# An adaLN block with windowed attention and routed experts: first tiles normalised on VectorE, products of zeros moved and widened in the first block, first steps of GpSimd and TensorE written out

## What is computed

```python
mod = (silu(c) @ wmod).reshape(4, 6, 1, 128)        # sa, ca, ga, sb, cb, gb
ga = (2 * (ga >= 0) - 1) * maximum(abs(ga), 0.25)   # gb likewise
h = layernorm(x) * (1 + ca) + sa
q, k, v = h @ Wq.T, h @ Wk.T, h @ Wv.T              # 16 heads, 4 KV heads, D = 64
scores = 30 * tanh((q @ k / 8) / 30)                # key j for query i: i - 128 < j <= i
x = x + ga * (softmax(scores) @ v @ Wo.T)
h = layernorm(x) * (1 + cb) + sb
x = x + gb * moe(h)                                 # top 1 of 8 experts, relu, 512 wide
```

## Time and profile before

| | us |
|---|---|
| median of 3 executions | 450.78 (450.40 to 451.82) |
| the profiled execution | 450.22 |
| its span, first to last instruction | 448.5 |
| TensorE busy | 422.5 (94% of the span) |
| VectorE busy | 293.8 (66%) |
| ScalarE busy | 300.1 (67%) |
| GpSimd busy | 310.1 (69%) |

### The profile page before, as it was taken

The page is one execution under the profiler, slowest core; times in us unless marked ns, Lnnn a source line. Parts: engine busy times, 40 slices in busy tenths (PEclk is TensorE's granted clock), DMA queues, the critical chain, the costliest instruction groups (busy, mean ns, idle before and its releaser), DMA issues. The chain is left out here.

```text
span 448.5 us, 14988 instructions
## 1 busy us (share of the span) xinstructions
PE 422.5 (94%) x5628; PEld 294.5 (66%) x5628; DVE 293.8 (66%) x878; ACT 300.1 (67%) x537; POOL 310.1 (69%) x495
## 2 busy tenths in 40 slices
PE   8899999999999999999999999999998856999991
PEld 4656767666767676676767675767655543799991
DVE  6475576766686868486767675775768662476751
ACT  5978586868786868777777777785856431555540
POOL 4546475868787878687878777786777884066663
PEclk9999999999999999999999999999999977899997
DMA  7663602101010210121212200202021033993110
GB/s 245 223 228 100 203 21 71 34 19 53 23 56 19 62 59 23 38 61 38 60 39 67 68 31 20 79 20 80 26 84 42 10 101 105 330 362 109 35 43 28
DMA packets 33023, 37.15 MB, mean 83 GB/s; under 512 B 3650, under 2 KB 29255, under 8 KB 32952
## 3 DMA queue, kind: packets, MB, share of 16 engines
q1 hardware_dynamic: 29448, 27.43, 20.2%
q0 software_dynamic: 3072, 8.37, 5.1%
q10 hardware_dynamic: 432, 0.40, 0.3%
HBM read 15.69 MB, written 16.91 MB: 73 GB/s over the span
## 5 line engine op out<-in xcount | busy, mean ns | idle before, releaser
L1071 DVE COPY_PREDICATED own<-before,turns 128x1024 f32<-128x1024 uint32 x56 | 68.8, 1229 | 42.6 <-PE turns L455 42.4
L1552 POOL TENSOR_TENSOR OL<-O,OH 128x512 fp32r<-128x512 f32 x64 | 81.8, 1284 | 17.5 <-ACT OH L826 17.3
L813 ACT ACTIVATE PR<-own 128x1024 f32<-128x1024 f32 x64 | 65.4, 1022 | 17.4 <-DVE own L1071 17.4
L1543 POOL TENSOR_SCALAR_AFFINE_SELECT PM<-PR 128x1024 f32<-128x1024 f32 x64 | 70.3, 1098 | 7.1 <-ACT PR L819 7.1
L819 ACT ACTIVATE PR<-PR 128x1024 f32<-128x1024 f32 x64 | 67.2, 1050 | 0.1
L451 PE MATMUL own<-Q,K 64*32 64x128 f32 (+3 forms) x896 | 58.7, 441 | 1.9 <-issue 1.4
L455 PE MATMUL turns<-Q,K 64*32 64x128 f32 (+3 forms) x896 | 57.4, 429 | 0.0
L1104 DVE TENSOR_TENSOR O<-turns,R 128x512 f32<-128x512 f32 x64 | 42.9, 682 | 16.2 <-PE turns L494 16.1
L1588 POOL DMA_INDIRECT sorted_rows<-PAY,slot_i x32 | 34.6, 1082 | 13.0 <-issue 12.4
L455 PEld LDWEIGHTS turns<-Q,K 64*32 64x32 f32 x896 | 36.6, 107 | 9.5
L799 ACT ACTIVATE Q<-turns 128x512 f32<-128x512 f32 x64 | 38.3, 600 | 5.5 <-PE turns L377 4.1
(11 more groups left out here) (201 smaller groups left out, 1041.3 us busy)
## 6 DMA issues: line engine op xcount, KB each, us to landing
sorted_rows<-empty_row SPq DMA_DIRECT2D x8, 776.0 KB, 6.5
VM<-V SPq DMA_DIRECT2D x56, 64.0 KB, 2.1
out_dram<-PAY SPq DMA_DIRECT2D x32, 64.0 KB, 1.8
w_stage<-w_dram SPq DMA_DIRECT2D x8, 256.0 KB
PR<-sorted_rows SPq DMA_DIRECT2D x2, 776.0 KB, 9.2
x_sb<-sorted_rows SPq DMA_DIRECT2D x2, 776.0 KB, 10.2
x_sb<-x_dram SPq DMA_DIRECT2D x3, 512.0 KB, 5.9
O<-w_dram SPq DMA_DIRECT2D x4, 256.0 KB, 8.5
```

Source lines behind the costliest of these rows:

```text
L813: act.activation(pr, own[:, :, :].rearrange("p a n -> p (a n)"), ACT.Tanh, scale=SCORE_SCALE).then_inc(tanhed, 1)
L1071: dve.copy_predicated(own[:, :, :].rearrange("p a (r n) -> p (a r) n", n=P), before[:, :].bitcast(U32).unsqueeze(1).to_broadcast([P, 2 * R ...
L1543: pool.affine_select(out=PM[:, u % P_RING, :].rearrange("p (r n) -> p r n", n=P), in_=PR[:, u % P_RING, :].rearrange("p (r n) -> p r n", n ...
L1552: pool.tensor_tensor(OL[:, t % 2, :, half], O[:, t % 2, :, half], OH[:, t % 2, :, half].bitcast(F32), ALU.subtract).then_inc(ol_done, 1)
```

## The change

Loads and splits: the second pair of tiles has a load of its own, ahead of the second half of the query weights; the value weights come after these. The output weights' high parts are made on VectorE (`split_both`) instead of ScalarE. First tiles: `normalise_first` on VectorE replaces `normalise1` for tiles 0 and 1, and GpSimd leaves out two of four steps for block 0. V of block 0 is copied by VectorE (`keep_v_first`), ahead of `prepare_mod`. `high_x(0)` comes ahead of the split of the first query weights. TensorE: zeros of 256 columns ahead of `turn_x(0)`, 384 instead of 128 columns ahead of `project_k(0)`, `project_q(0, 2)` ahead of `project_v(0)`. The first pass of TensorE's loop is written out, with `attend(0)` ahead of `turn_x(3)` and `score(1, 1)`, where the loop had it behind both. GpSimd's first steps are written out, with `mask(0, 0)` ahead of `rstd1_of(3)` and of `differ(1)`, and `mask(0, 1)` ahead of the last two `rstd1_of`. The measures of tiles 10 and 11 move ahead of VectorE's loop.

```diff
...
-            (WkH[:, :], WkL[:, :], stage_k), (WqH[:, :QH], WqL[:, :QH], stage_q[:, :QH]), (WvH[:, :], WvL[:, :], stage_v),
-            (WqH[:, QH:], WqL[:, QH:], stage_q[:, QH:]),
+            (WkH[:, :], WkL[:, :], stage_k), (WqH[:, :QH], WqL[:, :QH], stage_q[:, :QH]), (WqH[:, QH:], WqL[:, QH:], stage_q[:, QH:]),
+            (WvH[:, :], WvL[:, :], stage_v),
...
             sp.dma_start(stage_q[:, :QH], wq[:, :QH]).then_inc(wq0_in, 16)
+            sp.dma_start(x_sb[:, 2:4, :], x_v[0][:, 2:4, :]).then_inc(x_second, 16)
+            sp.dma_start(stage_q[:, QH:], wq[:, QH:]).then_inc(wq1_in, 16)
             sp.dma_start(stage_v, wv).then_inc(wv_in, 16)
-            sp.dma_start(stage_q[:, QH:], wq[:, QH:]).then_inc(wq1_in, 16)
-            sp.dma_start(x_sb[:, 2:BATCH_TILES, :], x_v[0][:, 2:BATCH_TILES, :]).then_inc(x_in[0], 16)
+            sp.dma_start(x_sb[:, 4:BATCH_TILES, :], x_v[0][:, 4:BATCH_TILES, :]).then_inc(x_in[0], 16)
...
+            run_idle(1, 2)
             pe.wait_ge(consts, CONSTS)
             turn_x(0)
...
-            run_idle(1, 1)
+            run_idle(1, 3)
             project_k(0)
             project_q(0, 1)
             project_q(0, 0)
+            project_q(0, 2)
             project_v(0)
-            project_q(0, 2)
             turn_x(1)
...
             score(1, 0)
+            project_v(1)
+            project_q(1, 3)
+            sums(0)
+            attend(0)
+            turn_x(3)
+            score(1, 1)
+            project_q(2, 1)
+            score(2, 0)
+            project_k(2)
+            sums(1)
+            project_q(2, 0)
+            score(2, 1)
+            attend(1)
+            project_q(2, 2)
+            score(3, 0)
-            for e in range(-10, TILES - 14, 2):
+            for e in range(-8, TILES - 14, 2):
...
             split_high(SPLIT_K)
-            normalise1(0)
-            normalise1(1)
+            high_x(0)
             split_high(SPLIT_Q0)
-            high_x(0)
-            split_high(SPLIT_V)
             act.wait_ge(rows_done, 1)
             act.activation(mod3_flat, bank["rows",][0:BATCHES, 0:3 * P], ACT.Copy).then_inc(mod_kept, 1)
             split_high(SPLIT_Q1)
+            split_high(SPLIT_V)
             keep_k(0)
...
             normalise1(3)
-            keep_v(0)
             high_x(1)
...
             normalise1(6)
-            split_high(SPLIT_O1)
-            split_high(SPLIT_O0)
+            normalise1(7)
             keep_v(1)
             weigh(1, 0)
-            normalise1(7)
             keep_q(1, 3)
...
+            def normalise_first(t):
+                dve.wait_ge(rstd1_done, 1)
+                dve.tensor_scalar(XN[:, t * P:(t + 1) * P], x_sb[:, t, :], mv1[:, t, 0:1], rstd1[:, t:t + 1],
+                                  ALU.subtract, ALU.mult).then_inc(normed1, 1)
+
+            def keep_v_first():
+                dve.wait_ge(v_projected, 1)
+                dve.tensor_copy(V[:, 0:2, :], bank["v", 0].rearrange("p (t n) -> p t n", t=2)).then_inc(v_kept, 1)
+
+            def split_both(i):
+                dve.wait_ge(split_in[i], 16)
+                dve.tensor_copy(split[i][0], split[i][2]).then_inc(weights_h, 1)
+                split_low(i)
...
             split_low(SPLIT_K)
+            normalise_first(0)
+            normalise_first(1)
             keep_columns()
             keep_gate()
-            split_low(SPLIT_Q0)
             full_x(0)
             low_x(0)
+            split_low(SPLIT_Q0)
             measure1(2)
             measure1(3)
             gather1(2)
             gather1(3)
+            split_low(SPLIT_Q1)
             split_low(SPLIT_V)
-            split_low(SPLIT_Q1)
             measure1(4)
...
             gather1(5)
+            keep_v_first()
             prepare_mod()
             full_x(1)
             low_x(1)
+            split_both(SPLIT_O1)
+            split_both(SPLIT_O0)
             measure1(6)
...
+            measure1(10)
+            measure1(11)
+            gather1(10)
+            gather1(11)
...
-                if e == 6:
-                    split_low(SPLIT_O1)
-                    split_low(SPLIT_O0)
...
-                pool.tensor_scalar(minus1[:, s], mv1[:, s, 0], -1.0, None, ALU.mult).then_inc(minus1_done, 1)
+                if k:
+                    pool.tensor_scalar(minus1[:, s], mv1[:, s, 0], -1.0, None, ALU.mult).then_inc(minus1_done, 1)
                 pool.wait_ge(var1_done, k + 1)
                 pool.tensor_tensor(rstd1[:, s], var1[:, s], neg_half[:, :], ALU.pow).then_inc(rstd1_done, 1)
+                if k == 0:
+                    return
...
-            for e in range(-12, TILES - 4, 2):
+            rstd1_of(0)
+            rstd1_of(1)
+            rstd1_of(2)
+            mask(0, 0)
+            rstd1_of(3)
+            differ(1)
+            mask(0, 1)
+            rstd1_of(4)
+            rstd1_of(5)
+            for e in range(0, TILES - 4, 2):
```

More of the change, by code:

```diff
@@ L189, in build @@
         turns = pb("turns", [P, 6, 512])
-        x_first = sem("x_first")
+        x_first, x_second = sems("x_first", "x_second")
         x_in = [sem(f"x_in{b}") for b in range(BATCHES)]
@@ L202, in build @@
         final_out = [sem(f"final_out{n}") for n in range(3)]
-        consts, banks_cleared, c_exped, c_steps, silu_done, columns_done, rows_done, mod_kept, sa_kept, ca_kept = sems(
-            "consts", "banks_cleared", "c_exped", "c_steps", "silu_done", "columns_done", "rows_done", "mod_kept", "sa_kept", "ca_kept")
+        consts, banks_cleared, c_steps, silu_done, columns_done, rows_done, mod_kept, sa_kept, ca_kept = sems(
+            "consts", "banks_cleared", "c_steps", "silu_done", "columns_done", "rows_done", "mod_kept", "sa_kept", "ca_kept")
         cb_kept, gate_parts, gates_kept, weights_h, weights_l = sems(
@@ L240, in build @@
         split = (
-            (WkH[:, :], WkL[:, :], stage_k), (WqH[:, :QH], WqL[:, :QH], stage_q[:, :QH]), (WvH[:, :], WvL[:, :], stage_v),
-            (WqH[:, QH:], WqL[:, QH:], stage_q[:, QH:]),
+            (WkH[:, :], WkL[:, :], stage_k), (WqH[:, :QH], WqL[:, :QH], stage_q[:, :QH]), (WqH[:, QH:], WqL[:, QH:], stage_q[:, QH:]),
+            (WvH[:, :], WvL[:, :], stage_v),
             (WoH[:, REP:, :], WoL[:, REP:, :], stage_o[:, REP:, :]), (WoH[:, :REP, :], WoL[:, :REP, :], stage_o[:, :REP, :]))
-        SPLIT_K, SPLIT_Q0, SPLIT_V, SPLIT_Q1, SPLIT_O1, SPLIT_O0 = range(6)
-        split_in = (wk_in, wq0_in, wv_in, wq1_in, wo_in, wo_in)
+        SPLIT_K, SPLIT_Q0, SPLIT_Q1, SPLIT_V, SPLIT_O1, SPLIT_O0 = range(6)
+        split_in = (wk_in, wq0_in, wq1_in, wv_in, wo_in, wo_in)
         CONSTS = 15
@@ L762, in normalise1 @@
                 k, j = divmod(t, 2)
-                act.wait_ge(shift1_done, k + 1)
-                if k:
-                    act.wait_ge(x_turned, k)
+                act.wait_ge(shift1_done, k)
+                act.wait_ge(x_turned, k)
                 act.activation(XN[:, j * P:(j + 1) * P], x_sb[:, t, :], ACT.Identity, bias=shift1[:, t:t + 1],
@@ L863, in program_act @@
             act.wait_ge(c_in, 16)
-            act.activation(c_e[:, :], cT[:, :], ACT.Exp, scale=-1.0).then_inc(c_exped, 1)
+            act.activation(c_e[:, :], cT[:, :], ACT.Exp, scale=-1.0).then_inc(c_steps, 1)
             split_high(SPLIT_K)
-            normalise1(0)
-            normalise1(1)
+            high_x(0)
             split_high(SPLIT_Q0)
-            high_x(0)
-            split_high(SPLIT_V)
             act.wait_ge(rows_done, 1)
@@ L1047, in measure1 @@
             def measure1(t):
-                dve.wait_ge(x_first if t < 2 else x_in[t // BATCH_TILES], 16)
+                dve.wait_ge(x_first if t < 2 else x_second if t < 4 else x_in[t // BATCH_TILES], 16)
                 if t >= 2:
@@ L1170, in prepare_silu @@
             def prepare_silu():
-                dve.wait_ge(c_exped, 1)
+                dve.wait_ge(c_steps, 1)
                 dve.tensor_scalar(c_e[:, :], c_e[:, :], 1.0, None, ALU.add).then_inc(c_steps, 1)
-                dve.wait_ge(c_steps, 1)
+                dve.wait_ge(c_steps, 2)
                 dve.reciprocal(c_r[:, :], c_e[:, :]).then_inc(c_steps, 1)
-                dve.wait_ge(c_steps, 2)
+                dve.wait_ge(c_steps, 3)
                 dve.tensor_tensor(siluT[:, :], cT[:, :], c_r[:, :], ALU.mult).then_inc(silu_done, 1)
@@ L1241, in program_dve @@
                     locate(e - 11)
-                if is_tile(e + 6):
+                if is_tile(e + 6) and e + 6 > 11:
                     measure1(e + 6)
@@ L1283, in program_dve @@
                     top8(e - 9)
-                if is_tile(e + 7):
+                if is_tile(e + 7) and e + 7 > 11:
                     measure1(e + 7)
@@ L1519, in rstd1_of @@
                 pool.tensor_scalar(var1[:, s], mv1[:, s, 1], EPS, 1.0, ALU.add, ALU.mult).then_inc(var1_done, 1)
-                pool.tensor_scalar(minus1[:, s], mv1[:, s, 0], -1.0, None, ALU.mult).then_inc(minus1_done, 1)
+                if k:
```

(5 more changed lines are left out.)

## The result

The changed kernel takes 454.26 us (median of 9, 451.42 to 455.94) against 450.52 us (median of 9, 448.73 to 451.82). The ratio is 1.0076, with a 95% interval from 1.0054 to 1.0097: slower, by some 3.4 us (the medians themselves are 3.7 apart). The forecast was 453.2, range 450.8 to 454.8.

A forecast was written before the change was run, and what follows sets the result against it. TensorE was taken as the bound, gapless from 34.9 to 332 us. On the profiled 450.22 us, 0.8 grown to 1.0 in the head and 2.0 for the order gave 453.2 us, range 450.8 to 454.8.

The forecast's parts named there:

- The bound: TensorE has no hole from 34.9 to 332 us, so the change is worth TensorE's shift at about 35 us.
- The order, +2.0: First block's attention: attend(0) ahead of turn and score(1,1) makes score(2,0) 2.36 late, 0.38 comes back: 2.0 us lost.
- The 0.38 that "comes back": Keys behind score(2,0), at 32.03: they waited for the scaling, now done in time, which returns 0.38 us.
- The head, +1.0: Stretch up to score(1,0): longer zeros cost 0.8, prepare_mod makes second keys 1.3 late, score(1,0) ends 1.0 us late.
- Two of the signs set for "right": Changed timeline: keys' first product at 10.4 or later, and second keys over 1 us later than 15.78.
- the same 10.4: Start of TensorE: its rise from 1.2 to 2.4 GHz taken to come at 10.4 us in both kernels.
- a faster normalisation can gain 0.1 at most: First turn: the columns' product, ending at 6.39, lets it start, not the normalised tiles, so at most 0.1 us gained.
- the 0.56: Profiled execution of the kernel before, 450.22, lies 0.56 us under the median 450.78; left to the range.
- VectorE's 1.0: Third block: VectorE's splits and measures could make full_x(2) late by up to 1.0 us; counted in the range's upper end.
- Early upper level: Rival, 0.22: extra zeros bring TensorE to 2.4 GHz before the turn at about 7 us, head about -0.1: 452.1.
- VectorE the bound: Rival, 0.08: VectorE's splits and measures are late for full_x(2) by up to 1.0 us: 454.2.
- The order at no cost: Rival, 0.12: attend(0) falls in a wait score(1,1) would have had anyway, so only the head counts: 451.2.

The follow-up runs named there:

- e3: Changed kernel with products of zeros in its two holes, ahead of attend(0) and behind score(1,1): 452.3 us, ratio 1.0025 to the kernel before.
- e1: Changed kernel with one part undone, score(1,1) ahead of attend(0) again: 448.71 us, ratio 0.9965 to the kernel before.
- e2: Kernel before with one part of the change alone, attend(0) ahead of turn_x(3) and score(1,1): 453.24 us, ratio 1.0065.
- e7: Kernel before, unchanged, profiled a second time: one execution, 452.02 us.
- e5: Changed kernel with score(1,1) ahead of attend(0) again and the products of zeros as before: 449.35 us, ratio 0.9967 to the kernel before.
- e4: Changed kernel with sums(0) in bank 5 instead of bank 1: one execution, 450.81 us.
- e9: e8 with the old zeros, one output-weight split behind merge(1,0), measures of tiles 10 and 11 behind the first turned sums: 448.85 us, ratio 0.9966.
- e6: e1 with VectorE's copy of V and prepare_mod behind the second block's full and low part: 451.12 us, ratio 1.0022 to the kernel before.
- e8: e6 with turn_x(2) ahead of score(0,1), high_x(2) ahead of weigh(0,1), full_x(2) and low_x(2) ahead of the output weights' splits: 448.33 us, ratio 0.9957.
- e10: Changed kernel, unchanged, profiled a second time: one execution, 456.56 us.

## Why the prediction was right, and where it was not

**The bound.** Right: what the timeline shows late at 39 us is late to the end of the attention (4.02 at 39, 4.00 at 361).

**The order, +2.0.** The hole ahead of score(2,0) was right in place, releaser and size: score(1,1) was to come 2.36 later relative to score(1,0) and came 2.35 later; TensorE idles 0.84 ahead of attend(0) and 1.9 ahead of score(2,0). One term was missing: the lower level that follows the hole. Score(2,0) takes 2.06 instead of 1.24, the keys behind it 1.58 instead of the 0.89 that they take in e3, 1.5 together; e3 gives 1.4 of this back. With it the distance grew by 3.46, against 2.0 forecast.

The 0.38 that "comes back" at the keys I put down to the lateness. e1 shows the same 0.38 without any lateness, and e2 has the lateness without it (its keys still wait 0.31 for the scaling): it came from the splits that left VectorE's loop. Against e1 the order costs 2.8 at the upper level.

**The head, +1.0.** The places were right (zeros, then prepare_mod ahead of the second low part). The size came out at 0.56, the second keys 0.91 late and not 1.3, but that compares one execution with one, and e7 alone moved score(1,0) by 1.29. Two of the signs set for "right" did not come: keys at 10.4 or later, second keys over 1 late. The step that failed is the forecast of "the same 10.4" for the rise and of the columns' end at 6.39. The columns began at 4.62 and not at 4.98 and were followed at 5.76, and the level was up before 9.96, so keys started at 9.56 and not at 10.5.

A second step failed beside it: "a faster normalisation can gain 0.1 at most". That was read from an execution whose columns had waited for their data. Three more profiles have their columns at the same 4.62 as the changed kernel, and at the lower level. In e2, with all first steps old, the turn then waits 0.64 for a normalised tile and stands at 6.62, the keys at 9.07. In e5, with the new steps and the old zeros, the turn follows the columns at 5.89 and the keys stand at 8.35. With the new zeros the keys are at 9.56 and, in e3, 9.60. So the new first steps gain 0.7 there, which was put at nothing, and the zeros cost 1.2. What is left of it at score(1,0) is 0.4 to 0.5 (21.74 in e2, 22.23 and 22.15 with the change).

**What the rest of the change is worth.** I gave it nothing. With the order back it is 0.35% faster than before (e1), of which the distance shows 0.8 in the first block. 0.18 of it is the mask and 0.38 the splits; the rest is the turn ahead of score(1,1), which before waited 0.19 for ScalarE. The other half of e1's gain would have to lie in the head. Executions scatter by more than that there, so it is not shown. So the sum had two errors of opposite sign beside the right one: the lower level too little, the rest of the change too dear. That the time still fell into the range is partly luck: its upper end had been set by the 0.56 and by VectorE's 1.0, not by a fall of the clock.

**Rivals.** Early upper level: seen in single executions (e1, e4, e9), all of them with the new first steps, but not from the cause that the rival names. In e1 the level was up at the columns' loads (4.89), ahead of the first new zeros at 5.66, and e9 has the old zeros. VectorE the bound: not in the changed kernel (0.16 of idling ahead of full_x(2)), but in e6. The order at no cost: refuted by e1 and e2.

**Open.** Whether the kernel before ever begins at the upper level: two profiles of it and e2 all begin low. Whether the new steps make an early rise likelier is not shown. The three profiles with the old first steps have their first short weight load at 10.5 or later (13.1 in e7), the nine with the new ones by 10.3; but they are one profile each of several kernels.

## What to carry to other kernels

Where TensorE is gapless later, look at what its list holds between a score and the next one: a long step moved from behind the score to ahead of it delays the score, and the same time comes back as the hole that the step used to fill. Count it once: attend(0) took 1.87 up to the next step and came back as the hole of 1.91, with the 0.84 for the bank on top. Price a hole like this one with the lower level behind it too (1.5 here), and read that from the weight loads and the granted clock. Before a term of the start is put at nothing, compare executions in which the start fell differently. When an edit closes a wait, write down the next entry of each engine's list before believing the gain: e6, e8 and e9 each closed theirs.

## What the runs showed of the hardware

TensorE falls to 1.2 GHz in the middle of otherwise dense work: the hole of 1.9 us (2.4 in e6) was followed by weight loads of 0.33 instead of 0.19 in five profiles of five (after, e2, e4, e6, e10), with a granted clock of 0.50 around them (0.57 in e6), and with zeros in its place (e3) they stayed at 0.19 and 1.00. In four of the five a shorter hole (0.84, in e4 0.45) stands some 4 us ahead of it; e3 filled both, so what the long one does alone is seen only in e6. The holes of 1.39 ahead of score(1,0) in the kernel before and e2 were not followed by a fall. The Trainium skill, "TensorE: Matmul & The Clock Gate", Part 1, has the clock set by how busy TensorE has been recently. The trace agrees (0.33 against 0.19), and it shows the fall behind a wait for a tanh, between a score and a score.

The start differs by over a microsecond between executions whose TensorE steps are the same up to there: behind the same 3.8 us of zeros the columns' weights arrive at the upper or the lower level (six loads 0.82 in e1, 1.35 in e5), and the columns' product began anywhere from 4.4 to 5.4. In one and the same kernel, the one before, the first short load stands at 10.5 in one profile and at 13.1 in the other. In this early part the granted clock of the table reads 1.00 while the loads take 0.33 (e7, 9.0 to 12.9), so there the loads are what tells the level.

VectorE's copy of 128x512 from SBUF took 0.42, where the subtraction of the same size took 0.69; the copy of 512 elements out of PSUM took 0.69 (the prediction had at most 0.68 for each).
